# A decoder layer on one core: the output norm's weight by one power, the router's weights and token numbers written by GpSimd, one-hot rows and slots in fused operations

## What is computed

```python
# attention, per head of 64 features: p is a softmax over 64 slots, hv the value states
p = jax.nn.softmax(logits, axis=-1)
o_t = jnp.einsum('bhm,bhmv->bhv', p, hv)
o = o * jax.lax.rsqrt(jnp.mean(o * o, axis=-1, keepdims=True) + NORM_EPS) * g_norm_w   # NORM_EPS = 1e-05
# router and experts
logits = jnp.clip(xf @ Wr, -CLAMP, CLAMP)
top_v, top_i = jax.lax.top_k(logits, 2)
expv = jnp.exp(top_v - m)                                        # m: the larger of the two
top_p = expv / (jnp.sum(expv, axis=-1, keepdims=True) + 1e-12)
oh = experts[:, None] == jnp.arange(E)[None, :]                  # one-hot rows
pos = jnp.sum(jnp.cumsum(oh.astype(jnp.int32), axis=0) * oh, axis=-1) - 1
kept = pos < cap                                                 # cap = 1280
xe = jnp.zeros((E, cap + 1, D), x.dtype).at[experts, pos_safe].set(xf[tokens])[:, :cap]
h = jax.nn.silu(jnp.einsum('ecd,edf->ecf', xe, W1)) * jnp.einsum('ecd,edf->ecf', xe, W3)
ye = jnp.einsum('ecf,efd->ecd', h, W2)
out = jnp.zeros((T, D), x.dtype).at[tokens].add(wk[:, None] * yp)
```

## Time and profile before

| | us |
|---|---|
| median of 3 runs | 1491.87 (1491.67 to 1504.76) |
| the profiled execution: device time | 1492.93 |
| the profiled execution: span, first to last instruction | 1491.2 |
| PE busy | 1371.4 (92%) |
| PEld busy | 1217.7 (82%) |
| DVE busy | 951.7 (64%) |
| ACT busy | 632.5 (42%) |
| POOL busy | 345.9 (23%) |

### The profile page before, as it was taken

How to read it: one execution, slowest core, us unless ns; L and a number is a source line. 1 busy time by engine, 2 the same in 40 slices (tenths; PEclk the granted TensorE clock), 3 DMA queues, 4 the chain that set the end, 5 groups by cost and what they waited for, 6 DMA issues and landing times. The chain is left out here.

```text
span 1491.2 us, 32495 instructions
## 1 busy us (share of the span) xinstructions
PE 1371.4 (92%) x10841; PEld 1217.7 (82%) x10841; DVE 951.7 (64%) x3164; ACT 632.5 (42%) x1594; POOL 345.9 (23%) x524
## 2 busy tenths in 40 slices
PE   5799999899998999999866999999999999999995
PEld 3667777677777777777646999999999999999995
DVE  4468888788787878878754645555554655555442
ACT  1255455445445445445333434444343434444331
POOL 3112223132222323223210112121121212221122
PEclk9699999999999999999957999999999999999998
DMA  5341031011000001000003142231424232242111
GB/s 162 85 137 48 19 116 32 17 31 30 17 30 31 26 20 31 29 17 27 22 21 120 30 114 37 59 91 30 114 40 117 33 110 35 42 113 33 30 23 22
DMA packets 67292, 79.67 MB, mean 53 GB/s; under 512 B 11090, under 2 KB 60723, under 8 KB 67154
## 3 DMA queue, kind: packets, MB, share of 16 engines
q1 hardware_dynamic: 52562, 59.09, 13.0%
q0 software_dynamic: 14592, 18.91, 7.7%
HBM read 44.04 MB, written 33.96 MB: 52 GB/s over the span
## 5 line engine op out<-in xcount | busy, mean ns | idle before, releaser
L837 ACT ACTIVATE h_a<-banks 128x256 f32<-128x256 f32 x320 | 122.4, 383 | 352.2 <-PE banks L1319 350.6
L1253 DVE TENSOR_TENSOR h_f<-banks,h_a 128x256 f32<-128x256 f32 x320 | 135.5, 423 | 152.0 <-ACT h_a L837 146.9
L551 POOL TENSOR_TENSOR idle_g<-half 128x1 f32<-128x1 f32 x144 | 29.7, 206 | 699.7 <-DVE y_s L1272 391.3
L1319 PE MATMUL banks<-xe_t_hi,w_even_hi 128*128 128x256 f32 x640 | 179.8, 281 | 0.0
L1319 PE MATMUL banks<-xe_t_hi,w_odd_hi 128*128 128x256 f32 x640 | 178.6, 279 | 0.0
L1319 PE MATMUL banks<-xe_t_lo,w_even_hi 128*128 128x256 f32 x640 | 177.9, 278 | 0.0
L1319 PE MATMUL banks<-xe_t_hi,w_even_lo 128*128 128x256 f32 x640 | 177.8, 278 | 0.0
L1319 PE MATMUL banks<-xe_t_lo,w_odd_hi 128*128 128x256 f32 x640 | 177.0, 276 | 0.0
L1319 PE MATMUL banks<-xe_t_hi,w_odd_lo 128*128 128x256 f32 x640 | 176.9, 276 | 0.0
L826 ACT ACTIVATE h_t_hi<-h_f 128x256 fp32r<-128x256 f32 x320 | 131.8, 412 | 32.4 <-DVE h_f L1253 32.4
L1260 DVE TENSOR_TENSOR h_t_lo<-h_f,h_t_hi 128x256 fp32r<-128x256 f32 x320 | 133.5, 417 | 9.6 <-ACT h_t_hi L826 5.3
(11 more groups left out here) (240 smaller groups left out, 3518.2 us busy)
## 6 DMA issues: line engine op xcount, KB each, us to landing
raw<-in_w SPq DMA_DIRECT2D x24, 1024.0 KB, 5.8
expert_rows<-empty SPq DMA_DIRECT2D x4, 2580.0 KB, 11.3
xe<-expert_rows SPq DMA_DIRECT2D x40, 258.0 KB, 2.8
xin<-in_x SPq DMA_DIRECT2D x32, 128.0 KB, 2.4
out_dram<-x SPq DMA_DIRECT2D x32, 128.0 KB, 1.8
out_dram<-y_s,token POOLq DMA_INDIRECT x80, 3.8
mask_i<-in_mask SPq DMA_DIRECT2D x32, 32.0 KB, 1.8
expert_rows<-r_xn,send POOLq DMA_INDIRECT x64, 3.1
```

What stands on the lines that cost most here:

```text
L551: return pool.tensor_tensor(idle_g[:, i:i + 1], half[:, 0:1], half[:, 0:1], ALU.add)
L837: act.activation(h_a[:, f % 2, :], bank[2 + f % 4][:, 0:GS], ACT.Silu).then_inc(silu_ok, 1)
L1253: dve.tensor_tensor(h_f[:, f % 2, :], bank[2 + f % 4][:, GS:2 * GS], h_a[:, f % 2, :], ALU.mult)\
L1319: last = pe.matmul(dst, lhs, rhs, start=(i == 0), stop=(i == len(pairs) - 1))
```

## The change

In the output norm, `b_rec` is gone. DVE forms `b_floor = 1e-5 * b_sum * b_sum` in one fused operation after `b_sum`, and `b_ms = b_ss/64 + b_floor` in another after the squares are reduced; the power -0.5 of it is `b_w` itself, written by POOL, since (ss/(64 sum^2) + eps)^(-1/2) / sum = (ss/64 + eps sum^2)^(-1/2). `b_t1`, `b_t2`, `b_ms`' old form and `b_w` on DVE go. In the routing, `hot` is one comparison of two broadcast operands, `base` goes into a fused `slot_f`, and `r_den`, `r_p` (now a power -1 with a new constant tile `neg_one`), the two weight columns and the token number move to the front of `send_rows` on POOL, before the wait for the slots; a second `hold` stands after it.

```diff
--- before
+++ after
-ROUTE_STEPS = 11
+ROUTE_STEPS = 7
+SEND_STEPS = 3
...
             def head_power(n, c, b):
-                power(n, b_ms, b_rms, ms_ok, rms_ok, bw_ok)
+                power(n, b_ms, b_w, ms_ok, bw_ok, bo_ok)
...
                 par = c % 2
                 if not later(n, 1):
                     pool.wait_ge(zeros_sent, 64)
+                pool.wait_ge(re_ok, n + 1)
+                hold(0)
+                pool.tensor_scalar(r_den[:, :], r_e[:, :], 1.0, 1e-12, ALU.add, ALU.add).then_inc(send_step, 1)
+                pool.wait_ge(send_step, n * SEND_STEPS + 1)
+                pool.tensor_tensor(r_p[:, :], r_den[:, :], neg_one[:, :], ALU.pow).then_inc(send_step, 1)
+                pool.tensor_copy(r_xn[:, par, :, D:D + 1],
+                                 token_no[:, bass.ds(n, 1)].rearrange("p (a b) -> p a b", b=1).to_broadcast([P, 2, 1]))
+                pool.wait_ge(send_step, n * SEND_STEPS + 2)
+                pool.tensor_tensor(r_xn[:, par, 1, D + 1:ROW], r_p[:, :], r_e[:, :], ALU.mult)
+                pool.tensor_copy(r_xn[:, par, 0, D + 1:ROW], r_p[:, :]).then_inc(send_step, 1)
                 pool.wait_ge(slots_ok, n + 1)
-                hold(0)
+                pool.wait_ge(r_normed, n + 1)
+                pool.wait_ge(send_step, n * SEND_STEPS + SEND_STEPS)
+                hold(5)
                 for k in range(2):
...
             def router_exp(n, c, b):
                 act.wait_ge(gap_ok, n + 1)
                 if later(n, 1):
-                    act.wait_ge(slots_ok, n)
+                    act.wait_ge(send_step, n * SEND_STEPS)
                 act.activation(r_e[:, :], gap[:, :], ACT.Exp).then_inc(re_ok, 1)
...
                 dve.wait_ge(bsum_ok, n + 1)
-                dve.reciprocal(b_rec[:, :], b_sum[:, :]).then_inc(brec_ok, 1)
+                dve.scalar_tensor_tensor(out=b_floor[:, :], in0=b_sum[:, :], scalar=EPS, in1=b_sum[:, :],
+                                         op0=ALU.mult, op1=ALU.mult).then_inc(floor_ok, 1)
...
             def head_squares(n, c, b):
 
                 dve.wait_ge(sq_ok, n + 1)
-                dve.tensor_reduce(b_ss[:, :], b_sq[:, :, :], AX.X, ALU.add).then_inc(rms_step, 1)
-                dve.wait_ge(rms_step, 3 * n + 1)
-                dve.wait_ge(brec_ok, n + 1)
-                dve.tensor_tensor(b_t1[:, :], b_ss[:, :], b_rec[:, :], ALU.mult).then_inc(rms_step, 1)
-
-            def head_squares2(n, c, b):
-                dve.wait_ge(rms_step, 3 * n + 2)
-                dve.tensor_tensor(b_t2[:, :], b_t1[:, :], b_rec[:, :], ALU.mult).then_inc(rms_step, 1)
-                dve.wait_ge(rms_step, 3 * n + 3)
-                if later(n, 1):
-                    dve.wait_ge(rms_ok, n)
-                dve.tensor_scalar(b_ms[:, :], b_t2[:, :], 1.0 / M, EPS, ALU.mult, ALU.add).then_inc(ms_ok, 1)
-
-            def head_weights(n, c, b):
-
-                dve.wait_ge(rms_ok, n + 1)
-                dve.tensor_tensor(b_w[:, :], b_rms[:, :], b_rec[:, :], ALU.mult).then_inc(bw_ok, 1)
+                dve.tensor_reduce(b_ss[:, :], b_sq[:, :, :], AX.X, ALU.add).then_inc(bss_ok, 1)
+                dve.wait_ge(bss_ok, n + 1)
+                dve.wait_ge(floor_ok, n + 1)
+                if later(n, 1):
+                    dve.wait_ge(bw_ok, n)
+                dve.scalar_tensor_tensor(out=b_ms[:, :], in0=b_ss[:, :], scalar=1.0 / M, in1=b_floor[:, :],
+                                         op0=ALU.mult, op1=ALU.add).then_inc(ms_ok, 1)
 
...
-                dve.tensor_copy(r_xn[:, c % 2, :, D:D + 1],
-                                token_no[:, bass.ds(n, 1)].rearrange("p (a b) -> p a b", b=1).to_broadcast([P, 2, 1]))
...
-                for k in range(2):
-                    dve.tensor_scalar(hot[:, k, :], expert_no[:, :], top_f[:, k:k + 1], None, ALU.is_equal)\
-                       .then_inc(route_step, 1)
-                dve.wait_ge(route_step, n * ROUTE_STEPS + 4)
+                dve.tensor_tensor(hot[:, :, :], expert_no[:, :].rearrange("p (a e) -> p a e", a=1).to_broadcast([P, 2, E]),
+                                  top_f[:, :].rearrange("p (k a) -> p k a", a=1).to_broadcast([P, 2, E]), ALU.is_equal)\
+                   .then_inc(route_step, 1)
+                dve.wait_ge(route_step, n * ROUTE_STEPS + 3)
                 if later(n, 1):
                     dve.wait_ge(cnt_mm, n)
                 dve.tensor_tensor(both[:, :], hot[:, 0, :], hot[:, 1, :], ALU.add).then_inc(both_ok, 1)
...
-                dve.tensor_scalar(base[:, :], top_f[:, :], float(CAP), None, ALU.mult).then_inc(route_step, 1)
-                dve.wait_ge(re_ok, n + 1)
-                dve.tensor_scalar(r_den[:, :], r_e[:, :], 1.0, 1e-12, ALU.add, ALU.add).then_inc(route_step, 1)
+                dve.wait_ge(route_step, n * ROUTE_STEPS + 4)
+                dve.tensor_reduce(pos[:, :], place_h[:, :, :], AX.X, ALU.add).then_inc(route_step, 1)
                 dve.wait_ge(route_step, n * ROUTE_STEPS + 5)
-                dve.tensor_reduce(pos[:, :], place_h[:, :, :], AX.X, ALU.add).then_inc(route_step, 1)
-                dve.wait_ge(route_step, n * ROUTE_STEPS + 7)
-                dve.reciprocal(r_p[:, :], r_den[:, :]).then_inc(route_step, 1)
-
-                dve.wait_ge(route_step, n * ROUTE_STEPS + 8)
                 dve.tensor_scalar(off_f[:, :], pos[:, :], float(CAP), SKIPPED, ALU.is_ge, ALU.mult)\
                    .then_inc(route_step, 1)
-                dve.tensor_tensor(slot_f[:, :], pos[:, :], base[:, :], ALU.add).then_inc(route_step, 1)
-
-                dve.wait_ge(route_step, n * ROUTE_STEPS + 9)
-                dve.tensor_copy(r_xn[:, c % 2, 0, D + 1:ROW], r_p[:, :])
-                dve.tensor_tensor(r_xn[:, c % 2, 1, D + 1:ROW], r_p[:, :], r_e[:, :], ALU.mult)
+                dve.scalar_tensor_tensor(out=slot_f[:, :], in0=top_f[:, :], scalar=float(CAP), in1=pos[:, :],
+                                         op0=ALU.mult, op1=ALU.add).then_inc(route_step, 1)
                 dve.wait_ge(route_step, n * ROUTE_STEPS + ROUTE_STEPS)
                 dve.tensor_tensor(send[:, c % 2, :], slot_f[:, :], off_f[:, :], ALU.add).then_inc(slots_ok, 1)
...
                 run(1, head_squares)
-                run(1, head_squares2)
                 run(2, x_maximum)
-                run(1, head_weights)
                 run(1, head_outputs)
```

More of the change, by code:

```diff
@@ L92, in decoder_layer @@
         half = sb("half", [P, P])
-        neg_half = sb("neg_half", [P, 4])
-        idle_v, idle_g = sb("idle_v", [P, 1]), sb("idle_g", [P, 3])
+        neg_half, neg_one = sb("neg_half", [P, 4]), sb("neg_one", [P, 1])
+        idle_v, idle_g = sb("idle_v", [P, 1]), sb("idle_g", [P, 6])
         before_experts = ExitStack()
@@ L169, in decoder_layer @@
         lg, lg_d, b_e = (part1(t, [P, H, M]) for t in ("lg", "lg_d", "b_e"))
-        lg_m, b_sum, b_rec, b_ss, b_t1, b_t2, b_ms, b_rms, b_w = (
-            part1(t, [P, H]) for t in ("lg_m", "b_sum", "b_rec", "b_ss", "b_t1", "b_t2", "b_ms", "b_rms", "b_w"))
+        lg_m, b_sum, b_floor, b_ss, b_ms, b_w = (
+            part1(t, [P, H]) for t in ("lg_m", "b_sum", "b_floor", "b_ss", "b_ms", "b_w"))
         b_p = part1("b_p", [P, D])
@@ L203, in decoder_layer @@
         pos = part1("pos", [P, 2])
-        base = part1("base", [P, 2])
         slot_f, off_f = part1("slot_f", [P, 2]), part1("off_f", [P, 2])
@@ L256, in decoder_layer @@
             "gates_mm less_ok gates_ok s_ok decay_mm h_ok ks_mm ks_ok sums_mm z_ok scores_mm a_ok")
-        logits_mm, lg_ok, lgm_ok, lgd_ok, be_ok, bsum_ok, brec_ok, bp_ok, p_mm, p_ok, mix_mm, mix_ok = sems(
-            "logits_mm lg_ok lgm_ok lgd_ok be_ok bsum_ok brec_ok bp_ok p_mm p_ok mix_mm mix_ok")
-        read_mm, sq_ok, rms_step, ms_ok, rms_ok, bw_ok, bo_ok, o_mm, o_ok, y_mm, x1_ok = sems(
-            "read_mm sq_ok rms_step ms_ok rms_ok bw_ok bo_ok o_mm o_ok y_mm x1_ok")
+        logits_mm, lg_ok, lgm_ok, lgd_ok, be_ok, bsum_ok, floor_ok, bp_ok, p_mm, p_ok, mix_mm, mix_ok = sems(
+            "logits_mm lg_ok lgm_ok lgd_ok be_ok bsum_ok floor_ok bp_ok p_mm p_ok mix_mm mix_ok")
+        read_mm, sq_ok, bss_ok, ms_ok, bw_ok, bo_ok, o_mm, o_ok, y_mm, x1_ok = sems(
+            "read_mm sq_ok bss_ok ms_ok bw_ok bo_ok o_mm o_ok y_mm x1_ok")
+        send_step = sem("send_step")
         x_stats, x_vared, x_rstded, x_normed, x_cols_mm, x_cols_ok, xq_mm, xq_ok = sems(
@@ L343, in is_last @@
             return isinstance(n, int) and n == last
-        CONSTS = 20 + XH
+        CONSTS = 21 + XH
         W_LOADS = 11 + B
@@ L500, in _ @@
             pool.memset(neg_half[:, :], -0.5).then_inc(consts_step, 1)
+            pool.memset(neg_one[:, :], -1.0).then_inc(consts_step, 1)
             pool.memset(taken[:, :], 0.0).then_inc(consts_step, 1)
@@ L519, in _ @@
                                    base=0, pattern=[[-w, n]], channel_multiplier=1).then_inc(consts_step, 1)
-            pool.wait_ge(consts_step, 13 + XH)
+            pool.wait_ge(consts_step, 14 + XH)
```

(2 more changed lines are left out.)

4 lines of the change are left out of this document (2 added, 2 removed).

## The result

| | before | after |
|---|---|---|
| median, us | 1497.26 (1489.46 to 1505.86, 8 runs) | 1513.0 (1503.71 to 1518.58, 8 runs) |
| profiled execution: span | 1491.2 | 1516.8 |
| of it, chunk stage (to the first product of the experts) | 794.1 | 805.8 |
| of it, expert stage | 697.1 | 711.0 |

The ratio is 1.0099, 95% interval 1.0068 to 1.0129: the change makes the kernel about 1% slower. Forecast were 1477.5 us and a range to 1486. The changed kernel's profiled execution was the longest of its eight and that of the kernel before one of the shorter ones, so these two spans differ by 25.6 us, the medians by 15.7; a second profile of the changed kernel (after_again) has 799.3 us of chunk stage and 708.0 of expert stage. In both stages time was lost, each for its own reason, and neither reason is in the work that was edited. The edited work itself behaves nearly as forecast, so I begin there.

A forecast was written before the change was run, and what follows sets the result against it. PE, 92% busy, was taken to bound the kernel, with its waits set by a ring over DVE, PE and ACT. Gains of 13.7 us from 1492.93 gave 1479.2, median 1478.2; forecast 1477.5 us, range 1471 to 1486.

The forecast's parts named there:

- The ring in a regular step: Chunk step without `keys` or round start: dependency cycle over DVE, PE and ACT, forecast 0.34 us shorter per step.
- The written-out steps 5 to 7: Chunk steps outside the loop: three times the regular step's 0.34 us, 1.0 us together.
- the sum: Loop 10.8 us (six rounds of 1.80), steps 5 to 7 1.0, steps 32 to 35 1.4, token column 0.5: 13.7 us.
- the limit: Regular step: ACT's `down` can come only 0.34 us earlier, though DVE could start `both` and `g_s` 0.78 earlier.
- In the first step of a round: Chunk loop: PE's 1.14 us wait for `both` exceeds DVE's 0.78, so this step gains the whole 0.78 us.
- PE's clock: Rival in the loop: clock falls may go (1474) or another come (1482); below 1474, ring giving more included, chance 0.12.
- what the chunk stage gains it gains whole: Expert stage: not edited, starts once the last rows have landed, so the chunk stage's gain passes through undiminished.
- The base: Starting time: profiled execution's device time 1492.93 us, with the median of the runs 1.1 below it.
- POOL's part: New work in `send_rows`: about 1.6 to 1.7 us, ready just ahead of the slots, costed at nothing.
- no stretched DVE operation beside it: Sign against the shared-port rival: `place_h` or `send` stretched beside POOL's work would show the forecast wrong.
- within 1%: Whole kernel: time within 1% (14.9 us) of no change, chance 0.53.
- the rivals that I had named: PE's clock (1474 or 1482); shared DVE and POOL port (1489; 1484 to 1490, 0.17); POOL late (1497; above 1490, 0.08).

The follow-up runs named there:

- after_again: The changed kernel run and profiled once more, nothing edited: 1509.04 us, ratio 1.0076 to the kernel before.
- norm_only: The kernel before with the output norm's edit alone, DVE's loop kept at instruction 642 by 54 repeated waits, tiles unmoved: ratio 0.9872.
- routing_only: The changed kernel with the output norm's edit taken back, DVE's loop at instruction 642, expert stage's tiles at their old places: ratio 0.9977.
- before_xe_32: The kernel before with one unused tile ahead of `xe`, so `xe`, `xe_t`, `h_t` and `y_s` stand 32 bytes higher: ratio 1.0107.
- before_32_bytes: The kernel before with one unused tile more, which moves all tiles behind it up by 32 bytes, no instruction added: ratio 1.002.
- the repaired kernels: The changed kernel with DVE's loop at instruction 642 and the constant -1 in `neg_half`'s tile, tiles at old places: 0.9922 (1488.67 us), repeated 0.9951.
- after_8_later: The changed kernel with 16 repeated waits on DVE, so its loop begins at instruction 594 instead of 586: ratio 1.0047.

## Why the prediction was wrong

- **The ring in a regular step: right, a little low.** Forecast 0.34 us; measured 0.47 and 0.36. `down` follows `one_less` by 0.31 us in all 32 steps; what gives the 0.1 more in the one step was not looked into. The written-out steps 5 to 7 gave 21.92 to 21.55, 1.1 us for 1.0. The first step behind a branch, without the second stall and without a fall of the clock, went from 20.52 to 19.88: 0.64 for 0.78. The last of a round 24.16 to 23.84: 0.32 for 0.34. Together 1.8 us per round, as in the sum, but in five rounds and not six: the first step of the loop's first round, which follows no branch and where `down` already stood 0.31 behind `one_less`, gained nothing, and that round 1.0. norm_only shows the limit at work as the prediction had it; routing_only, where 0.20 was expected and 0 and 0.17 came, does so in one step only.
- **The step that failed in the chunk stage: "In the first step of a round".** It took the stall behind the branch from the rows as a thing that the change leaves alone ("PE stays idle before f_norm whatever the change does"), and so put the code's position at nothing. It isn't nothing, since the change shortens the code ahead of the loop by 56 instructions. Instead of 0.78 us less, each of the five first steps took 2.8 us more, 14.2 us together (23.82 against 20.98 in the mean; 23.37 and 12.0 us in after_again), more than the loop's whole gain. With the start put back, the chunk stage of the full change, in seven executions whose loop begins at 610 or 642, takes 778.4 to 787.9 us (mean 783.5), against 794.1, 794.0 and 801.5 (mean 796.6) for the kernel before with its own start: -13.1 us, where -13.7 was forecast. That they are so close is in part luck: 1.5 us of the 13.1 lie ahead of step 5, where nothing was forecast; the loop up to its last step gave 9.0 for 10.5, steps 5 to 7 gave 1.1 for 1.0, and the last step of the loop with all that follows it 1.4 for 1.7. Advanced Engine Details and Errata of the Trainium skill (ISA Cache) bears on this: it gives two cache lines of 16 KB, 256 instructions each. The trace agrees that code comes in blocks; the 8 KB packets and the distance of 128 between the two bad starts say half that size for DVE. The same page of the Trainium skill (Control Flow Timing) puts a compare-and-branch at about 108 ns. No run here shows such an amount: DVE's branch back is followed by 2.3 us or more without work.
- **The rival "PE's clock" had the right place and too small a price.** It allowed for another fall (1482). What came were falls at all five starts, behind 3.1 to 3.3 us of idle time on PE where the kernel before has 1.4 to 1.7 and one fall.
- **Another fall, in step 2, is not the change's.** That step took 26.2 to 26.5 us instead of 21 to 22 in 7 of the 20 profiled executions (granted clock 0.68 between 70 and 90 us in before_xe_32, 0.95 in the kernel before), among them the changed kernel's two, before_32_bytes and before_xe_32.
- **The step that failed in the expert stage: "what the chunk stage gains it gains whole".** An unedited stage was taken for an unchanged one. The new tile moved its tiles by 32 bytes; it took 13.9 us more (10.9 in after_again). How much of that is the place and how much the chance of the execution is not settled: the kernel before, at its own places, varies too.
- **The base.** The profiled execution of before had no slow group; medians of before in the six comparisons are 1496.3 to 1501.8 us, not 1491.87. The forecast as a ratio, 0.990, is what the repaired kernels come near (0.992 and 0.995); in us it was 11 too low even for them (1488.67).
- **Right at no cost:** POOL's part (1.63 us for 1.6 to 1.7), the place of `send`, no stretched DVE operation beside it (`place_h` and `send` at most 0.02 us longer), PE's waits for `g_s` down from 27 to 7.
- **The chances.** By the ratio, 1.0099, the result just falls into "within 1%", to which I gave 0.53; but that case was made up of gains below 1%, so this is luck. The chance of 0.02 for slower by over 1% counted only the rivals that I had named, and both causes were outside of them.

## What to carry to other kernels

A loop on an engine has a position in that engine's code. Adding or removing instructions ahead of it can cost more than the edit gains, so look at the first rows behind the branch for "issue" in the changed kernel before judging the edit, and try it with a few idle instructions ahead. Where a stage bound by PE lies behind it, a small new constant is better put into a free column of an old tile, so that no tile of that stage moves. Where an unedited stage changes its time, compare it group by group first.

## What the hardware showed unexpectedly

- DVE's return to the loop's start costs 2.3 to 2.7 us in every kernel here but after_8_later, where it costs 3.3 to 3.4, and 1.6 to 1.9 us more come seven or eight instructions later where the loop begins at 586 or 714.
- One and the same product over 256 columns goes at 276, 280 or 283 ns, at a granted clock of 1.00, by the place of its operands: none, 32 or 64 bytes of shift between activations and weights.
- Behind 2.4 to 3.4 us of idle time on PE at a round's start the clock fell to 1.2 GHz in 25 of 25 cases, behind 1.4 to 1.8 us in 34 of 75.
